# A two-layer graph and recurrence kernel: 24 recurrence turns inside the count stage and 41 full turns behind it, in place of 25, 3 rough and 42 full; the last block's root placed earlier

## The reference

```python
h = layernorm(x) @ W + b                      # 3125 nodes, 256 channels
agg = segment_sum(h[src], dst); deg = count(dst)
x = x + agg / max(deg, 1)                     # 53125 edges
z = layernorm(x)                              # the 3125 nodes are now a sequence
i, g, o = z @ U_i + b_i, z @ U_c + b_c, z @ U_o + b_o
for t in range(3125):                         # one state of 256, strictly in order
    i_t = sigmoid(i[t] + h @ V_i); g_t = tanh(g[t] + h @ V_c); o_t = sigmoid(o[t] + h @ V_o)
    c = h * c + i_t * g_t                     # the old part is h * c; the f gate is not used
    h = o_t * tanh(c)
    out[t] = x[t] + h
```

## Time and profile before

| | us |
|---|---|
| median of 3 runs | 520.42 |
| lowest, highest | 519.9, 520.51 |
| profiled execution: its span, and its own time | 520.4 |
| TensorE busy in it | 428.4 (82%) |
| VectorE busy | 371.6 (71%) |
| ScalarE busy | 358.8 (69%) |
| GpSimd busy | 176.9 (34%) |

### The profile page before, as it was taken

How to read it: one execution, slowest core, us unless ns; L and a number is a source line. 1 busy time by engine, 2 the same in 40 slices (tenths; PEclk the granted TensorE clock), 3 DMA queues, 4 the chain that set the end, 5 groups by cost and what they waited for, 6 DMA issues and landing times.

```text
span 520.4 us, 15606 instructions
## 1 busy us (share of the span) xinstructions
PE 428.4 (82%) x6160; PEld 372.2 (72%) x6160; DVE 371.6 (71%) x1195; ACT 358.8 (69%) x931; POOL 176.9 (34%) x322
## 2 busy tenths in 40 slices
PE   2476899978899999999999999956777778888880
PEld 2254677867788888888888888845767667777770
DVE  2776999987887768668677335353677778888883
ACT  0342698456776677677767745567799989999980
POOL 4443500254444446446445334201222222222220
PEclk9996799999999999999999999986599999999996
DMA  3334000330000001000000010010000000100111
GB/s 117 138 105 123 1 2 31 104 104 15 28 24 1 1 15 38 1 3 29 23 3 1 13 39 1 2 50 1 3 3 3 4 3 4 52 25 31 54 52 55
DMA packets 9293, 16.92 MB, mean 33 GB/s; under 512 B 1694, under 2 KB 7139, under 8 KB 9214
## 3 DMA queue, kind: packets, MB, share of 16 engines
q1 hardware_dynamic: 7658, 13.32, 7.6%
q10 hardware_dynamic: 676, 1.67, 0.8%
q0 software_dynamic: 880, 0.86, 0.7%
HBM read 6.23 MB, written 9.61 MB: 30 GB/s over the span
## 4 chain that ended last, share of the span: by engine, by line
PE 38%; DVE 29%; ACT 11%; issue 8%; POOL 7%; DMA 5%; DVEq 0%; SPq 0%; ACTq 0%; POOLq 0%
PE bank L1128 10%; PE bank L1205 7%; PE bank L1097 7%; PE bank L1099 6%; DVE hots L1465 6%; DMA x_sb<-in_x_dram 5%; ACT tc L921 4%; DVE h L1660 3%; DVE h L1704 3%; PE bank L1051 3%; ACT gate L907 3%; DVE c_st L1655 3%; POOL rstd L634 2%; PE bank L1145 2%; POOL newton L633 2%
## 5 line engine op out<-in xcount | busy, mean ns | idle before, releaser
L1205 PE MATMUL bank<-h,V 128*128 128x63 f16 (+1 forms) x3096 | 109.9, 195 | 28.4 <-DVE h L1660 25.2
L1205 PEld LDWEIGHTS bank<-h,V 128*128 128x128 f16 x3096 | 101.3, 99 | 40.2 <-issue 33.6
L1051 PE MATMUL bank<-hots 128*128 128x125 f16 x625 | 120.8, 223 | 0.0
L1465 DVE TENSOR_TENSOR hots<-iota,kp 128x1024 f16<-128x1024 f16 x157 | 105.6, 698 | 19.9 <-PE bank L1051 16.9
L1097 PE MATMUL bank<-h_flat,counts 125*128 125x257 f16 x375 | 97.3, 273 | 0.4 <-ACT counts L776 0.4
L1099 PE MATMUL bank<-h_flat,counts 125*128 125x256 f16 x375 | 96.4, 271 | 0.0
L633 POOL TENSOR_SCALAR newton<-rstd,var_eps 125x1 f32<-125x1 f32 x48 | 33.3, 694 | 119.8 <-DVE rstd L1537 117.4
L776 ACT ACTIVATE counts<-bank 125x500 f16<-125x500 f32 x96 | 55.2, 607 | 20.6 <-PE bank L1051 19.1
L665 POOL TENSOR_TENSOR hc<-h_flat,c_st 128x126 f32<-128x126 f32 x82 | 35.0, 426 | 101.0 <-DVE c_st L1655 99.0
L1097 PE MATMUL bank<-h_flat,gx 125*128 125x257 f16 x250 | 68.2, 274 | 0.0
L1099 PE MATMUL bank<-h_flat,gx 125*128 125x256 f16 x250 | 67.4, 270 | 0.0
(11 more groups left out here) (168 smaller groups left out, 814.6 us busy)
## 6 DMA issues: line engine op xcount, KB each, us to landing
h_dram<-h_flat SPq DMA_DIRECT2D x1, 3137.2 KB
x_dram<-x_sb SPq DMA_DIRECT2D x5, 625.0 KB
out_dram<-x_sb SPq DMA_DIRECT2D x4, 625.0 KB
x_sb<-in_x_dram SPq DMA_DIRECT2D x3, 625.0 KB
x_sb<-in_x_dram ACTq DMA_DIRECT2D x2, 625.0 KB
out_dram<-x_sb SPq DMA_DIRECT2D x1, 375.0 KB
gx<-in_L_gnn_weight_dram ACTq DMA_DIRECT2D x1, 256.0 KB, 4.2
gx<-in_L_ffn_U_i_dram SPq DMA_DIRECT2D x1, 256.0 KB, 2.7
```

Of the source, the lines that this page charges most:

```text
L1051: nc.tensor.matmul(ps_count[group % 3][:, pos * KEYS:(pos + 1) * KEYS], hots[:, ring, 0, g // 2, :, g % 2], hots[:, ring, 1, g // 2, 0:KEY ...
L1205: mm = nc.tensor.matmul(to[:, (m - m0) * n:(m - m0 + 1) * n], V16[:, v_part, d, m * P:(m + 1) * P], h16[:, h_part, d, c0:c1], start=False, ...
L1465: nc.vector.tensor_tensor(hots[:, k % RING, :, :, :, :].rearrange("p a h n g -> p (a h) n g"), iota[:, :, :].unsqueeze(1).to_broadcast(of) ...
```

## The change

FIRST_GROUP becomes 2, so warm-up is 40 turns and DONE is 65; HIDDEN becomes 24. The groups of steps are worked in the order 2, 3, 4, 0, 1 (x1's stores and the window thresholds follow it), and the hidden turn that ends a round is 15 instead of 20; the one behind the count stage is 40 instead of 45. Turns 21 to 23 use both parts of V on the rounded state (16 + 8 matmuls), and turn 24 all three products (24 + 12); its i and g gates are issued in two pieces, with the last block's first gate matmuls between them. Turns 20 to 23 also write the exact state into h_start, which GpSimd's old part now reads; turns 23 and 24 write a low part of the state. The out gate of a turn from 21 on waits for the exact state of the turn before. Turn 25 at places 650 to 658 is gone, and so are the three rough turns with VectorE's out seeds. Turns 25 to 65 are full; ScalarE seeds the out gate of the first too. The norm of the last block, and with it `last_root`, goes from place 636 to 632 on VectorE, ahead of turn 23's cell at 634. The wait for h_dram's store goes from behind the count stage into turn 24's exact state. The two instructions that read the covered edges move behind the first full turn. What is left out of the diff: two semaphores, the general path's order of seeds, and a simplification of the states at a round's end.

```diff
@@ -22,9 +22,10 @@
 STEPS = 25
-FIRST_GROUP = 1
-HIDDEN = 25
-ROUGH = 28
+FIRST_GROUP = 2
+HIDDEN = 24
+SHARP = 21
+FULL = 24
@@ -396,13 +399,14 @@
         SUM_AFTER = 4
+        assert FULL == HIDDEN
         FINISH_AT, NORM_AT, TURN_AT, HIGH_AT, LOW_AT = 36, 55, 53, 54, 63
...
-        LAST_AT = {FINISH_AT: (583, 605, 630), NORM_AT: (597, 616, 636), TURN_AT: (600, 618, 637),
+        LAST_AT = {FINISH_AT: (583, 605, 630), NORM_AT: (597, 616, 632), TURN_AT: (600, 618, 637),
                    HIGH_AT: (601, 619, 638), LOW_AT: (604, 621, 640)}
-        PLACES_END = 670
+        PLACES_END = 650
@@ -441,13 +445,23 @@
         E_SEED, E_PRODUCTS, E_GATE, E_OUT, E_OUT_GATE, E_TANH, E_CELL, E_STATE = 1, 5, 6, 11, 12, 15, 16, 25
-        LAST_PARTS = {E_SEED: 0, E_PRODUCTS: 1, E_GATE: 2, E_CELL: 3, E_OUT: 4, E_OUT_GATE: 5, E_TANH: 6, E_STATE: 8}
-        LAST_TURNS = {21: 609, 22: 620, 23: 631, 24: 637, 25: 650}
+        E_LOW = 26
+        LAST_PARTS = {E_SEED: 0, E_PRODUCTS: 1, E_GATE: 2, E_CELL: 3, E_OUT: 4, E_OUT_GATE: 5, E_TANH: 6, E_STATE: 8,
+                      E_LOW: 10}
+        LAST_TURNS = {21: 609, 22: 620, 23: 631}
...
+        FULL_PARTS = {E_SEED: 637, E_PRODUCTS: 638, E_LOW: 640, E_GATE: 641, E_CELL: 642, E_OUT: 643, E_OUT_GATE: 644,
+                      E_TANH: 644, E_STATE: 646}
...
             for t in range(1, HIDDEN + 1):
-                if w == (LAST_TURNS[t] + LAST_PARTS[part] if t in LAST_TURNS else (t + 3) * BLOCKS + 5 + part):
+                if t == FULL:
+                    at = FULL_PARTS[part]
+                else:
+                    at = LAST_TURNS[t] + LAST_PARTS[part] if t in LAST_TURNS else (t + 3) * BLOCKS + 5 + part
+                if w == at:
                     return t
@@ -640,9 +654,11 @@
                     pool.wait_ge(e_start, 2)
+                elif t >= SHARP:
+                    pool.wait_ge(e_h, t - SHARP + 1)
                 else:
                     pool.wait_ge(e_hi, t - 1)
-                nc.gpsimd.tensor_tensor(hc_w, h16[:, 0, :, :], c_st[:, c_before(t), :, :], ALU.mult).then_inc(e_hc, 1)
+                nc.gpsimd.tensor_tensor(hc_w, h_start[:, :, :] if t >= SHARP else h16[:, 0, :, :], c_st[:, c_before(t), :, :], ALU.mult).then_inc(e_hc, 1)
@@ -665,19 +681,15 @@
-            pool.wait_ge(e_hi, HIDDEN)
+            pool.wait_ge(e_h, HIDDEN - SHARP + 2)
             for t in range(HIDDEN + 1, DONE + 1):
                 n = t - HIDDEN
-                if t <= ROUGH:
-                    for q in range(2):
-                        if n > 1:
-                            pool.wait_ge(hi_ready[q], n - 1)
-                        old_part(q, h16[:, 0, :, :], c_before(t))
-                    continue
                 for q in range(2):
-                    pool.wait_ge(c_ready[1 - q], n - 1 + q)
-                    pool.wait_ge(h_ready[q], n - 1)
+                    if n - 1 + q > 0:
+                        pool.wait_ge(c_ready[1 - q], n - 1 + q)
+                    if n > 1:
+                        pool.wait_ge(h_ready[q], n - 1)
                     old_part(q, h_before(t), c_before(t))
@@ -841,6 +853,8 @@
                 act.wait_ge(e_ps, 2 * t - (1 if m0 == 0 else 0))
+                if m0 > 0 and t >= SHARP:
+                    act.wait_ge(e_h, t - SHARP + 1)
                 nc.scalar.activation(gate_w[:, m0:m1, :],
@@ -925,6 +939,7 @@
                 seed_ig(q, at_gx(HIDDEN + 1))
+                seed_o(q, at_gx(HIDDEN + 1))
             for t in range(HIDDEN + 1, DONE + 1):
@@ -936,16 +951,6 @@
-                if t <= ROUGH:
-                    gate_ig(0, n)
-                    gate_ig(1, n)
-                    gate_o(1, n)
-                    gate_o(0, n)
-                    tanh_c(0)
-                    next_ig(0)
-                    tanh_c(1)
-                    next_ig(1)
-                    continue
                 for q in range(2):
@@ -1140,12 +1145,25 @@
                         pe.wait_ge(e_hi, t - 1)
+                whole_ig = t == FULL and m0 == 0
+                parts = PRODUCTS[:1] if t < SHARP else PRODUCTS[:2] if t < FULL or whole_ig else PRODUCTS
+                for v_part, h_part in parts:
+                    mm = early_product(m0, m1, v_part, h_part)
+                if not whole_ig:
+                    mm.then_inc(e_ps, 1)
+            def early_product(m0, m1, v_part, h_part):
                 for m in range(m0, m1):
                         mm = nc.tensor.matmul(ps_early[:, (m - m0) * CHUNKS:(m - m0 + 1) * CHUNKS],
-                                              V16[:, 0, d, m * P:(m + 1) * P], h16[:, 0, d, :], start=False,
+                                              V16[:, v_part, d, m * P:(m + 1) * P], h16[:, h_part, d, :], start=False,
                                               stop=(d == HH - 1), skip_group_check=True)
-                mm.then_inc(e_ps, 1)
+                return mm
+            def early_low():
+                pe.wait_ge(e_lo, 1)
+                early_product(0, 2 * HH, *PRODUCTS[2]).then_inc(e_ps, 1)
@@ -1168,6 +1186,8 @@
                     early_products(t, 0, 2 * HH)
+                if w == FULL_PARTS[E_LOW]:
+                    early_low()
                 t = early_turn(w, E_OUT)
@@ -1208,26 +1228,22 @@
-            def rough_products(q, n):
-                pe.wait_ge(ig_seed[q], n)
-                if n > 1:
-                    pe.wait_ge(hi_ready[q], n - 1)
-                else:
-                    pe.wait_ge(e_hi, HIDDEN)
-                multiply(q, 0, 2 * HH, ps_g[q], PRODUCTS[0], True).then_inc(ig_ps[q], 1)
-                pe.wait_ge(o_seed[q], n)
-                multiply(q, 2 * HH, MT, ps_x[q], PRODUCTS[0], True).then_inc(o_ps[q], 1)
             def full_products(q, turn, hi_seen, lo_seen):
                 pe.wait_ge(ig_seed[q], turn)
-                pe.wait_ge(hi_ready[q], hi_seen)
+                if isinstance(hi_seen, int) and hi_seen == 0:
+                    pe.wait_ge(e_hi, HIDDEN)
+                else:
+                    pe.wait_ge(hi_ready[q], hi_seen)
                 for part in PRODUCTS[:2]:
...
-                pe.wait_ge(lo_ready[q], lo_seen)
+                if isinstance(hi_seen, int) and hi_seen == 0:
+                    pe.wait_ge(e_lo, 2)
+                else:
+                    pe.wait_ge(lo_ready[q], lo_seen)
                 multiply(q, 0, 2 * HH, ps_g[q], PRODUCTS[2], True).then_inc(ig_ps[q], 1)
@@ -1247,10 +1263,7 @@
                 for q in range(2):
-                    if t <= ROUGH:
-                        rough_products(q, n)
-                    else:
-                        full_products(q, n, n - 1, n)
+                    full_products(q, n, n - 1, n)
                     for step, d in out_parts(t, q):
@@ -1610,6 +1623,19 @@
+            def early_exact(t):
+                if t == HIDDEN:
+                    dve.wait_ge(line_stored, 16)
+                to = h_after(t) if t == HIDDEN else h_start[:, :, :]
+                nc.vector.scalar_tensor_tensor(out=to, in0=gate_w[:, 2 * HH:MT, :], scalar=1.0, in1=tc_w,
+                                               op0=ALU.add, op1=ALU.mult).then_inc(e_h, 1)
+                if t + 1 < FULL:
+                    return
+                dve.wait_ge(e_hi, t)
+                dve.wait_ge(e_h, t - SHARP + 2)
+                nc.vector.tensor_tensor(h16[:, 1, :, :], to, h16[:, 0, :, :], ALU.subtract).then_inc(e_lo, 1)
             UV_LOW = {64: 0, 71: 1, 77: 2, 83: 3, 90: 4, 97: 5}
@@ -1641,6 +1667,11 @@
                     early_state(t)
+                t = early_turn(w, E_LOW)
+                if SHARP - 1 <= t < FULL:
+                    early_exact(t)
+                if w == FULL_PARTS[E_STATE]:
+                    early_exact(FULL)
@@ -1660,25 +1691,14 @@
-            def seed_o(q, t):
-                c0, c1 = COLS[q]
-                n = c1 - c0
-                if t > HIDDEN + 1:
-                    dve.wait_ge(o_gate[q], t - 1 - HIDDEN)
-                nc.vector.tensor_copy(ps_x[q][:, 0:HH * n].rearrange("p (m k) -> p m k", k=n),
-                                      gx[:, slice(at_gx(t), at_gx(t) + 1), 2 * HH:MT, c0:c1]).then_inc(o_seed[q], 1)
             def state_next(q, t):
...
                 dve.wait_ge(tc_ready[q], t - HIDDEN)
-                full_next = t >= ROUGH
-                by = ROUGH - HIDDEN if t == ROUGH else 1
                 if not ends_round(t):
                     state(q, h16[:, 0, :, c0:c1], n).then_inc(hi_ready[q], 1)
-                    if full_next:
-                        state(q, h[:, :, c0:c1], n).then_inc(h_ready[q], by)
+                    state(q, h[:, :, c0:c1], n).then_inc(h_ready[q], 1)
                     return
@@ -1722,41 +1742,23 @@
-            dve.wait_ge(line_stored, 16)
             dve.wait_ge(sum_ps, BLOCKS)
             link(nc.vector.memset(h_start[:, :, 0:1], 0.0))
-            dve.wait_ge(bits_set, 1)
-            dve.wait_ge(gx_ready, MT * len(BATCHES))
             for q in range(2):
```

(53 more changed lines are left out.)

## The result

The changed kernel takes 506.53 us (506.28 to 506.67, 4 runs) where the kernel before took 520.46 beside it: a ratio of 0.9723 (95% interval 0.9704 to 0.9742). Measured once more it took 506.26 against 521.34, ratio 0.9716 (0.970 to 0.9732). The forecast was 506.2, the range 503.8 to 509.5.

A forecast was written before the change was run, and what follows sets the result against it. TensorE bounds to about 343 us, nobody is full between, the 3.22 us recurrence from 377.9. First full turn at 360.4 plus 145.7 gives 506.1 (14.3 off 520.4), stated as 506.2; range 503.8 to 509.5.

The forecast's parts named there:

- Part 1, the turns: Behind the count stage: turns 25 to 65, all full, 3.22 us each; from S to the end 145.7 us.
- S: Time at which the first full turn, turn 25, begins its products behind the count stage; forecast at 360.4 us.
- Part 2, the added products: Turns 21 and 22, ahead of the last sum: 24 more matmuls at 0.055 us delay the last block's finish 1.32 us.
- F: Start of the last block's finish, forecast 344.49; as rival: neighbouring-state test fails, all repeated, 10 ms, chance 0.02.
- Part 3, the exact states: VectorE, turns 20 to 23: exact states of 0.42 us each; no cost taken, though port hold-ups could add some 0.7 us.
- Part 4, the moved root: Last block's root ahead of cell 23: norm at 348.8, 0.4 us earlier; turn 24 begins at 351.8, 1.65 us later.
- Part 5, turn 24 to S: Turn 24 in full, replacing turns 24 and 25: from its start at 351.8 to first full turn's products at 360.4.
- A: As summed: the clock is back at 1.00 before S and holds, 506.2 us; chance 0.50.
- B: The clock is low at S, which becomes 361.7, and two full turns pay 1.6 us: 509.0; chance 0.28.
- C: Clock never falls at 348; 36 cold matmuls of turn 24 and the gates save 1.8 us: 504.3; chance 0.12.
- D: Extra work of turns 21 to 23 costs double by queueing, 508, or none of the 1.32, 504.8; chance 0.06.
- E: Slower: the clock does not come back in the full turns; 539 with all 41 low; chance 0.02.

## Why the prediction was right, and where it was not

**Part 1, the turns.** Right. 3.22 us a turn, 145.38 us from S where 145.7 was forecast; five turns in the shorter warm-up alone gave 16.10.

**Part 2, the added products.** Right: 1.32 forecast, 1.35 measured, all of it ahead of the last finish. F itself was 0.47 earlier than forecast because the two traces differ upstream. The finish of the first block has its reciprocal at 67.77 in before and at 66.88 in after, 0.89 earlier; one later interval of after is 0.17 shorter (9.59 for 9.76, which one other trace shows too); and after lost 0.57 at the round's end that had moved into a denser stretch. That last one is a term that the sum lacked altogether.

**Part 3, the exact states.** Free as forecast up to the finish. The hold-up on the port that I weighed and left out does exist (1.16 for 0.69, 0.88 for 0.4, 0.97 for 0.65), but in after it fell on no instruction that the chain went through behind 344 us; in the kernels with the clock up it does.

**Part 4, the moved root.** The step was right: norm before cell 23, 1.0 us earlier than before, state 23 decided by ScalarE; turn 24 was forecast 7.31 us behind the finish and came 7.34. The forecast had the out products of turn 23 at the low clock, and so they were in that trace; in the second, where they ran at the full one, it was 6.94. The move is worth 0.5 us up to turn 24 at like clock, 0.3 up to S.

**Part 5, turn 24 to S.** Mis-sized: 8.6 us forecast, 7.86 measured in both traces. I took 1.17 us from the last gx copies to the next seed from the old kernel, but it held 0.37 us of waiting; here it is 0.89 (357.89 to 358.78). The other 0.4 is the place of these copies: forecast 6.95 us behind turn 24's start (358.75), behind TensorE's last gate matmuls, they began 6.53 behind it (357.89), right behind the tanh; about half of that is turn 24's gate, 0.2 us sooner than forecast. (The price of a low matmul, 0.104 us, was read a little high: 12 from 351.28 to 352.51 are 0.1025 each. It changes nothing here: the low products came 2.89 behind turn 24's start where 2.95 was forecast.)

**The sum.** 506.1 was forecast for a span and 504.6 came: 0.5 from F, 0.7 from Part 5, 0.3 from S on. The time of 506.53 fits 506.2 because the span lacks 1.9 us of the time. So the hit on the time is partly luck: two errors of 1.5 and 1.9 us against each other. The saving forecast, 14.3, is right by the medians (13.9 and 15.1) by the same luck: in the spans, for which it was worked out, it was 15.8.

**The rivals.** A came true in both traces of after. B did not show in 8 runs of after. The rule of the Trainium skill (TensorE: Matmul & The Clock Gate, Part 1), that the point of the change varies from run to run, agrees with the traces: the same kernel had 0.53 and 0.76 in 348 to 355, and a kernel without fillers 1.00. It did not make pairs 3 us apart, though; F to S moved by 0.4. C's price was right in size (1.8 forecast, 1.4 measured with the clock held). D did not come: the added products cost 1.35, neither double nor nothing. E and F did not come either.

What stays open: why before and after differ by about 1 us ahead of the first block. It isn't the change. The windows of before and after:

```profile
60.00:70.00 10.00, 9.02 (x67) 7.26 (x65) 8.90 (x30) 8.10 (x20) 0.00 (x0) 0.75 0.01 2
```

```profile
60.00:70.00 10.00, 7.61 (x70) 5.83 (x68) 9.80 (x32) 8.54 (x21) 0.00 (x0) 1.00 0.01 2
```

In all thirteen traces the two go together. Four have a clock of 0.73 to 0.76 there and the first block's reciprocal at 67.6 to 68.2: before, the shorter warm-up alone, and two kernels made from after (without V's low part, tanh ahead of the seed). The other nine, before with fillers among them, have 0.97 to 1.00 and 66.5 to 67.0. So it goes by the execution and not by the kernel, and 0.9 us of the 15.8 between the two spans are of this kind. That the low clock is its cause is likely and not shown: no run held it there.

## What to carry to other kernels

Behind a full stage, count a removed turn at its period and measure it in a stretch of many; the boundary between two stages must be walked instruction by instruction, on all engines, and there a move is worth what the next wait leaves of it. Compare intervals inside a trace, not positions, when executions differ upstream by 1 us. Check what lies between the span and the time before a sum is made against it.

## What the runs showed of the hardware

TensorE's mean clock in the same 7 us of the same kernel was 0.53 in one execution and 0.76 in another; holding it with fillers took 1.4 us off where products and gates wait for each other, and 2 us off the old kernel. Early in the kernel, thirteen traces fall into two groups 1 us apart by the clock in 60 to 70 us. Fillers must stand ahead of a wait that ends early enough: behind it, 11 of them cost 0.6 us a turn. VectorE instructions on 250 elements a partition took 0.41 to 0.43 us; the low part of turn 23's state, which starts with GpSimd's old part in every trace, took 0.88, and GpSimd's old part took 0.97 instead of 0.63 where a VectorE instruction had just started; the Trainium skill (SBUF — State Buffer, on the shared port pair) says that such instructions exclude each other, and these durations agree.
